# Layer norms whose factor comes from a logarithm and an exponential on ScalarE instead of a root and a VectorE reciprocal, in a fused four-layer transformer kernel

## The reference

```python
def _ln(x, g, b, eps=1e-05):
    m = jnp.mean(x, axis=-1, keepdims=True)
    v = jnp.var(x, axis=-1, keepdims=True)
    return (x - m) * jax.lax.rsqrt(v + eps) * g + b
# layer 0: 16 heads
x = _ln(x + self_attention(x, causal=True), ln1_g, ln1_b)      # "n1" in the kernel
x = _ln(x + cross_attention(x, ctx), ln2_g, ln2_b)             # "n2"
x = _ln(x + gelu(x @ ff_W1.T + ff_b1) @ ff_W2.T + ff_b2, ln3_g, ln3_b)   # "n3"
# layer 1: 4 heads, self attention, SwiGLU, cross attention, SwiGLU, no normalisation
# layer 2: RMS norms ("r1", "r2"), a gated recurrence over 100 steps, 8-head cross attention, gelu MLP
# layer 3: one softmax attention over ctx, a projection, tanh
```

## Time and profile before

| | |
|---|---|
| median of 3 runs | 1568.34 us |
| the profiled execution | 1566.5 us, of which the profile's span is 1564.8 us |
| TensorE busy | 1476.2 us, 94% of the span |
| VectorE busy | 787.8 us, 50% |
| ScalarE busy | 668.4 us, 43% |
| table loads on ScalarE | 49 (by the program), 1283 ns each |
| TensorE's granted clock, mean of the span | 0.987 of 2.4 GHz |

### The profile page before, as it was taken

The page is one execution under the profiler, slowest core; times in us unless marked ns, Lnnn a source line. Parts: engine busy times, 40 slices in busy tenths (PEclk is TensorE's granted clock), DMA queues, the critical chain, the costliest instruction groups (busy, mean ns, idle before and its releaser), DMA issues.

```text
span 1564.8 us, 28689 instructions
## 1 busy us (share of the span) xinstructions
PE 1476.2 (94%) x12202; PEld 947.2 (61%) x12202; DVE 787.8 (50%) x1599; ACT 668.4 (43%) x1401; POOL 263.6 (17%) x443
## 2 busy tenths in 40 slices
PE   9888899898989999999999999999899999989998
PEld 8555565555555556555677765554566666655576
DVE  1677777867724266211233332324677777752132
ACT  2565556656545343111244432225544444443343
POOL 1433301010000000000022220000244544510000
PEclk9999999999989999999999999999899999999999
DMA  4311000000000020000200000000000000020032
GB/s 161 104 53 46 11 28 2 2 1 2 2 28 1 0 82 1 21 0 0 81 1 1 1 1 27 0 1 7 27 2 2 2 2 2 2 80 0 1 96 61
DMA packets 19562, 36.85 MB, mean 24 GB/s; under 512 B 2058, under 2 KB 17386, under 8 KB 18282
## 3 DMA queue, kind: packets, MB, share of 16 engines
q1 hardware_dynamic: 19434, 35.01, 6.7%
HBM read 33.36 MB, written 1.64 MB: 22 GB/s over the span
## 4 chain that ended last, share of the span: by engine, by line
PE 84%; DVE 9%; ACT 6%; issue 1%; DVEq 0%; ACTq 0%
PE psum L443 38%; PE psum L835 11%; PE psum L493 8%; PE psum L589 6%; PE psum L629 5%; ACT probs L1175 3%; DVE maxima L1515 3%; PE psum L585 3%; PE psum L528 2%; PE psum L940 2%; PE psum L968 1%; DVE t L1643 1%; PE psum L949 1%; PE psum L933 1%; PE psum L981 1%
## 5 line engine op out<-in xcount | busy, mean ns | idle before, releaser
L1515 DVE TENSOR_REDUCE maxima<-psum 100x2 f32<-100x722 f32 (+3 forms) x332 | 245.5, 760 | 109.7 <-PE psum L528 92.9
L443 PE MATMUL psum<-x_resid,weights 128*128 128x400 f32 x832 | 293.4, 503 | 3.7 <-ACT probs L1175 1.7
L443 PEld LDWEIGHTS psum<-x_resid,weights 128*128 128x128 f32 x832 | 156.5, 191 | 121.3 <-issue 3.8
L1175 ACT ACTIVATE probs<-psum 128x800 f32<-128x800 f32 (+3 forms) x224 | 168.0, 787 | 100.1 <-PE psum L589 99.4
L835 PE MATMUL psum<-weights 128*128 128x400 f32 x512 | 174.8, 499 | 0.7 <-DVE maxima L1515 0.7
L443 PE MATMUL psum<-weights,ctx_t 128*128 128x256 f32 (+1 forms) x576 | 155.6, 394 | 1.3 <-DVE max_rows L1526 0.7
L835 PEld LDWEIGHTS psum<-weights 128*128 128x128 f32 x512 | 97.2, 190 | 75.1 <-DVE maxima L1515 0.8
L493 PE MATMUL psum<-ctx_t,weights 128*128 128x361 f32 x384 | 137.5, 483 | 2.1 <-DVE weights L1770 0.8
L1097 ACT ACTIVATE weights<-psum 128x400 f32<-128x400 f32 (+2 forms) x80 | 37.9, 475 | 205.5 <-PE psum L443 205.4
L443 PEld LDWEIGHTS psum<-weights,ctx_t 128*128 128x128 f32 (+1 forms) x576 | 99.1, 184 | 41.3 <-issue 9.1
L629 PE MATMUL psum<-probs,values 128*32 128x100 f32 (+5 forms) x3328 | 113.1, 255 | 2.7 <-ACT q_then_o L1097 1.8
(11 more groups left out here) (163 smaller groups left out, 2117.1 us busy)
## 6 DMA issues: line engine op xcount, KB each, us to landing
weights<-in_w SPq DMA_DIRECT2D x2, 3072.0 KB, 10.3
staged<-in_ctx SPq DMA_DIRECT2D x32, 128.0 KB, 2.1
values<-in_ctx SPq DMA_DIRECT2D x32, 128.0 KB, 2.2
weights<-in_w SPq DMA_DIRECT2D x3, 1024.0 KB, 5.1
weights<-in_src SPq DMA_DIRECT2D x1, 2368.0 KB, 13.4
weights<-in_w SPq DMA_DIRECT2D x1, 2048.0 KB, 8.0
weights<-in_tw SPq DMA_DIRECT2D x2, 1024.0 KB, 5.2
staged<-in_ctx SPq DMA_DIRECT2D x16, 105.0 KB, 2.1
```

The source lines that it names most:

```text
L443: i = nc.tensor.matmul(PS[0:rows, bk, 0:n], lhs, rhs, start=k == 0, stop=k == len(terms) - 1)
L1175: nc.scalar.activation(PT[0:kn, k % PROBS_KEPT, :, 0:n], PS[0:kn, bk:bk + 2, 0:n], ACT.Exp).then_inc(act_results, mark("act", f"{t} p{b} { ...
L1515: nc.vector.reduce_max(top, src, AX).then_inc(dve_results, mark("dve", f"{t} m{b} {j}"))
```

## The change

Eight of the chains that have roots among exponentials (`n1` of all four groups, `n2` of groups 0 to 2, `n3` of group 3) compute the factor otherwise: ScalarE takes the logarithm of variance + eps, waits for its own result, and takes the exponential of -0.5 times it. VectorE's reciprocal falls away in these eight, and VectorE waits for ScalarE's `rs` instead. The other twelve chains with a root keep root and reciprocal. Ahead of `s0` and ahead of `s1` ScalarE loads by hand a table that holds logarithm and exponential together; in the attention stages `s0`, `c0` and `s1` all exponentials are then taken from that table. The program has 34 table loads after the change, where it had 49.

```diff
+        def by_logarithm(n, g):
+
+            return n == "n1" or (n == "n2" and g < NG - 1) or (n == "n3" and g == NG - 1)
...
             eps = 0 if n[0] == "n" else 1
+            if by_logarithm(n, g):
+                nc.scalar.activation(T2[:, g % 2, 0, :], PS[:, bank(f"{n} var{g}"), 0:N], ACT.Ln, bias=EPS[:, eps:eps + 1]).then_inc(act_results, mark("act", f"{n} root{g}"))
+                if due(f"{n} root{g}"):
+                    act.wait_ge(act_results, at(f"{n} root{g}"))
+                nc.scalar.activation(T2[:, g % 2, 0, :], T2[:, g % 2, 0, :], ACT.Exp, scale=-0.5).then_inc(act_results, mark("act", f"{n} rs{g}"))
+                return
             nc.scalar.activation(T2[:, g % 2, 0, :], PS[:, bank(f"{n} var{g}"), 0:N], ACT.Sqrt, bias=EPS[:, eps:eps + 1]).then_inc(act_results, mark("act", f"{n} root{g}"))
...
             if due("biases"):
                 act.wait_ge(dve_results, at("biases"))
 
+            nc.scalar.preload_act_table_set("natural_log_exp_and_others")
             act_attention(act, "s0", iter(()))
             act_attention(act, "c0", iter(()))
             act_feed(act, "f0")
+            nc.scalar.preload_act_table_set("natural_log_exp_and_others")
             act_attention(act, "s1", iter(()))
...
         def dve_scale(dve, n, g):
-            if due(f"{n} root{g}"):
-                dve.wait_ge(act_results, at(f"{n} root{g}"))
             rs = T2[:, g % 2, 0, :]
-            nc.vector.reciprocal(rs, rs).then_inc(dve_results, mark("dve", f"{n} rs{g}"))
+            if not by_logarithm(n, g):
+                if due(f"{n} root{g}"):
+                    dve.wait_ge(act_results, at(f"{n} root{g}"))
+                nc.vector.reciprocal(rs, rs).then_inc(dve_results, mark("dve", f"{n} rs{g}"))
             if due(f"{n} rs{g}"):
-                dve.wait_ge(dve_results, at(f"{n} rs{g}"))
+                dve.wait_ge(producer(f"{n} rs{g}"), at(f"{n} rs{g}"))
```

## The result

Before 1569.01 us, after 1554.28 us (medians of 4 executions each): ratio 0.9904, interval 0.9892 to 0.9917. The kernel is 14.7 us faster where 10.6 were forecast; 1554.28 lies at the lower edge of the wide range given (1554 to 1563.5) and outside that of the likeliest case (1555 to 1560); the gain of 14.7 us taken from the 1568.34 that the forecast started from is 1553.6. The profiled execution took 1554.73 us, with a span of 1553.0.

The account below looks back on a forecast made before the run. TensorE was taken to bound the kernel (busy 1476.2 of 1564.8 us), so only its waits count. 1.16 + 1.91 + 3.2 + 3.5 + 0.94 - 0.10 = 10.6 us, from 1568.34 to 1557.7; likeliest 1555 to 1560, 8 in 10 1554 to 1563.5.

Parts of the forecast that it names:

- groups 1 and 2 of `s0`: Product behind the late exponentials starts without idle time, because other products cover the load; gain 0 for two chains.
- end of `c0`, the turn at 427: Turn of the maxima (L559) waits 0.60 us for the bank the root frees; gain 0.30 us (bounds 0, 0.60).
- end of `c0`, waits (b) and (c): L585 waits: (b) 1.78 us for `max_rows` behind the reciprocal, gain 1.78; (c) 2.05 for exponentials behind the load, gain 1.13.
- end of `c0`, clock: TensorE's clock, at half from 433.2 to 443.0, stays at 1.00; gain 3.5 us (bounds 0 and 3.7).
- The step on `s1`: Waits of 0.38, 0.30 and 0.26 us vanish, gain 0.94 (bounds 0.3 and 0.94); load costed at nothing.
- from `f0` on nothing changes but that it starts sooner: Stages from `f0` on: claimed to start sooner and otherwise stay unchanged; no gain of their own in the sum.
- The judgement that the clock holds at the end of `c0`: End of `c0`: with waits of about 0.9 and 1.0 us left, the clock holds, "but not safely".
- The rival of a clock that falls all the same: Clock still falls at the end of `c0` or elsewhere instead: gain 7.1 us, time 1561.2; chance 0.22.
- The rival of waits that become others: Removed waits become other waits, as VectorE's list in `c0` is full: gain 3 us, time 1565.3; chance 0.08.
- Slower exponentials: New table slower per element in `s0`, `c0`, `s1`; at 30% slower the time is about 1571 us; chance 0.04.
- the rival that nothing changes: Whole program: the change does nothing measurable because loads remain; chance 0.02.
- No chain gets longer: Changed chains: VectorE's factor comes 0.7 us sooner where the load to the root stood, 3.3 us with the reciprocal.

## Why the prediction was right and wrong

The mechanism was right: the exponentials no longer stand behind a load, nor the maxima behind a reciprocal, and TensorE's idle time goes at the places named. The size was too small: places that were put at nothing gained, and the clock fell less often elsewhere too. By its own steps, the gain in us, predicted against the steps of the lag in the traces of the changed kernel:

| step | predicted | measured |
|---|---|---|
| the start | -0.10 | -0.10 to -0.11 in four traces without a fall there |
| groups 1 and 2 of `s0` | 0 | 0.41 + 0.42 |
| last group of `s0` | 1.16 | 1.41 |
| first three groups of `c0` | 1.91 | 0.73 + 0.58 + 0.59 = 1.90 |
| end of `c0`, the turn at 427 | 0.30 | 0.49 |
| end of `c0`, waits (b) and (c) | 2.9 | 1.8 to 2.2 |
| end of `c0`, clock | 3.5 | 3.9 if it holds |
| `s1` | 0.94 | 1.62 |

The split of the two last rows on `c0`: 5.76 us are gained when the clock holds, of which 10.2 us at half clock in the kernel before make 10.2 x 0.39 = 4.0; three other traces of the old code, with the 10.2 us in two pieces as the new kernel has its 6.8, took 0.44 to 0.50 us more than the earlier trace rows, hence up to 2.2. With the clock held the table gives 12.0 us, against 10.7 predicted for the same places.

- **The step on groups 1 and 2 of `s0`** failed on its rule that a product without a bracket is worth nothing. In the earlier trace rows the product starts 2.98 us after the eight before it began (91.12 to 94.10); in the profile after the same distance is 2.79 (91.93 to 94.72). Its 0.19 us of waiting carry no bracket; some more come behind it, 0.41 in all up to the next turn.
- **The step on `s1`** mis-sized the load by hand, "costed at nothing": it takes a load from between the squares and the exponentials into a stretch in which ScalarE waits for VectorE, and brings 1.42 of the 1.62 us alone, in a kernel without a single logarithm.
- **The main miss is the sentence "from `f0` on nothing changes but that it starts sooner"**, and with it that the clock counts at one place only. From the mean granted clock of each execution, (1 - clock) x 2 x span, the kernel before spends 42 us at half clock (mean of 76 executions), the changed kernel 25 (9 executions), and of the 17 us less the end of `c0` and the start of `f0` make about 7 (10.2 us in each of eight traces with the old chain there, 3.4 us on average in six with the new). Within one kernel, over 159 executions of all kernels here, a us at half clock goes with 0.24 us of time. The 17 us less are then some 4.2 us of gain. Waits of 8.0 to 8.5 us (the table without the clock) and 4.2 make 12.2 to 12.7, of the 14.7 to 16.4 measured; at the price of 0.39 it would be 14.7 to 15.1. By the steps of the lag a fall costs 0.26 us per us at 39.5 (1.77 for 6.8), 0.33 at 1119 (3.32 for 10.2) and 0.50 at 187 (1.69 for 3.4), so the 17 us can be worth 4 to 8.5. The measured gain is inside what this leaves, and how it divides isn't shown more closely.
- **The judgement that the clock holds at the end of `c0`** was half right: it held in three of six traces with the changed chain and fell for 3.4 us in three, while it fell for 6.8 or 10.2 us in all nine with a load ahead of the exponentials there. The rival of a clock that falls all the same gave 1561.2; its fall is a third as long as that rival assumed. Of the two halves of the change it is the load that goes with the fall: the clock fell in the kernel with the load and without the reciprocal and held in the one trace of the kernel without the load and with the reciprocal. Without the load it held in four traces of seven, so that a load makes the fall longer and likelier, and its absence does not rule one out.
- **The rival of waits that become others** did not come: the waits for maxima went to 0.59. **Slower exponentials** neither: two of 128x800 take 1.56 us in the profile after as in the earlier trace rows, and the rival that nothing changes fell with the loads gone.
- **The price of a load** is 1.28 us with nothing behind it: the three in a row above begin 1.29 us apart, and the exponential begins 1.30 us after the last of them did. "ScalarE: Activation LUTs", What ACT_TABLE_LOAD costs, in the Trainium skill has 2.66 us for a switch; by that, as an estimate, three loads less the idle time of 1.21 would have moved the exponentials by 6.8 us. The trace doesn't agree: the folded weights ended at 40.37 and the exponentials began at 44.27, 3.9 us later, where it had been 1.2, so that they moved by 2.7.
- **"No chain gets longer", and the factor 0.7 us sooner,** failed in `s0`. The step counted the load to the root as part of the chain. But that load doesn't wait for the variance, the root behind it does (13.2 us of idle time over 20 roots in the earlier trace rows), and so the load runs mostly while the variance is still being made. In the kernel before, at the second group of `s0`, the root ends at 89.37, 0.24 us behind the turn at 89.13, by the two rows below; in the profile after, the exponential ends 0.50 behind the same turn (at 90.45 and 89.95; its rows are the last of this document). The factor is 0.26 later there, and 0.25 is what the kernel with the reciprocals kept lost behind that chain. So in `s0` the chain is shorter by the reciprocal alone. At the first chain of `c0` the factor is 0.58 sooner (1.84 ahead of the turn at 239.34 before, 2.42 after).

```profile
87.49 1.28 ACT L1196 ACT_TABLE_LOAD   x1
88.78 0.59 ACT L1196 ACTIVATE t<-psum,eps 128x400 f32<-128x400 f32 x1
```

What stays open is what decides, in a stage that a change doesn't touch, whether the clock falls. The fall near 1110 to 1130 stands in 9 of 16 traces, with either kernel; a shift of 1.42 us brought 3.3, shifts of 2.7 and 3.9 cost 3.4 more than themselves. The kernels whose only difference is one or more loads show that such a surplus comes without a logarithm. Whether the position of the work in time decides it, or the idle time that the loads add or take, is not shown, and no more is the rule behind it.

## What to carry to other kernels

Read the idle time of the bounding engine from the distances of its starts, too: small waits carry no bracket and occur at every group. A table load belongs where its engine is idle anyway, and ahead of the wait of what follows, not behind it; that is one line, and at `s1` it brought 1.42 of the 1.62 us. Whether a load stands in a chain at all is read from what the engine waits for behind it: a load that runs while its function's input is still being made costs little there. Where the clock falls at several places, count a few us on either side for what a shift does to the falls behind it, and take the size of a small change from several executions and from steps of the lag at the place, not from the median alone.

## What the runs showed of the hardware

TensorE's clock fell to 1.2 GHz for 3.4, 6.8 or 10.2 us at a time, at 6 to 12 places of a trace (the one at its very end left out), and not at the same ones in two executions of one kernel. One fall came with TensorE hardly idle, in the changed kernel right behind the folding of the weights. The engine was busy for all of the 3.40 us ahead of it, and for 6.61 of the 7.00 us around it:

```profile
35.80:39.20 3.40, 3.40 (x43) 3.02 (x42) 1.08 (x6) 1.79 (x4) 0.00 (x0) 1.00 0.00 0
```

```profile
39.00:46.00 7.00, 6.61 (x46) 4.74 (x39) 1.89 (x2) 3.79 (x7) 3.39 (x4) 0.51 0.83 306
```

A reader of its own result waited next to nothing on ScalarE: the exponential of the logarithm begins 0.04 us after it ends.

```profile
89.28 0.59 ACT L1201 ACTIVATE t<-psum,eps 128x400 f32<-128x400 f32 x1 [1.00 <-PE psum L447]
89.91 0.54 ACT L1204 ACTIVATE t<-t 128x400 f32<-128x400 f32 x1
```
